# Five transposes of each group leave TensorE: 32x32 blocks turned on VectorE and put in place by DMA through memory, with a new order on every engine

## The reference, cut to what matters

```python
x = layernorm(x + L0(x, adj))   # attention, 8 heads of 16: softmax(q k / 4 + w_e[h] * adj, where adj != 0) v, then W_o
x = layernorm(x + L1(x))        # conv1 -> relu -> 17-tap conv2 -> relu; exp(-distance) @ relu(message); a GRU cell of both
x = layernorm(x + L2(x, adj))   # h = W x + b; adj * exp(e_i + f_j), rows divided by their sums, times h
x = layernorm(x + L3(x, adj))   # graph attention, 4 heads of 32: softmax(leaky(e_i + e_j), where adj > 0) h
```

## Time and profile before

| | |
|---|---|
| median of the executions | 1429.45 us (1429.4 to 1431.82) |
| profiled execution | 1432.08 us, span 1430.3 us |
| mean granted TensorE clock | 0.976 of full speed |
| TensorE matmul busy | 1352.1 us, 95% of the span |
| VectorE busy | 1191.3 us, 83% |
| ScalarE busy | 1188.4 us, 83% |
| GpSimd busy | 663.1 us, 46% |
| DMA | 46.86 MB, 33 GB/s over the span |

### The profile page before, as it was taken

One profiled execution on the slowest core, in us unless ns is written; L12 is line 12 of the kernel. 1 busy time (PEld: TensorE's weight loads), 2 busy tenths in 40 slices (PEclk: granted clock), 3 DMA queues, 4 the chain that ended last, 5 costly groups with the idle time before them and its releaser, 6 DMA issues.

```text
span 1430.3 us, 40514 instructions
## 1 busy us (share of the span) xinstructions
PE 1352.1 (95%) x13178; PEld 1075.1 (75%) x13267; DVE 1191.3 (83%) x3407; ACT 1188.4 (83%) x4353; POOL 663.1 (46%) x1014
## 2 busy tenths in 40 slices
PE   4799999999999999999999999999999999999964
PEld 3577788877778887777888777788877778887642
DVE  6568888888888888888888888888888888886763
ACT  3867888889888888998888899888889988887654
POOL 1133445554444555444455544445554444555532
PEclk7899999999999999999999999999999999999986
DMA  3100110011111001111100111111011111100000
GB/s 117 38 31 31 31 31 17 16 39 38 39 38 39 25 16 39 38 38 39 39 29 12 39 39 38 38 39 34 6 39 39 38 39 38 33 8 16 9 15 23
DMA packets 23825, 46.86 MB, mean 33 GB/s; under 512 B 2753, under 2 KB 2754, under 8 KB 23490
## 3 DMA queue, kind: packets, MB, share of 16 engines
q1 hardware_dynamic: 23618, 44.27, 9.8%
HBM read 35.88 MB, written 8.39 MB: 31 GB/s over the span
## 4 chain that ended last, share of the span: by engine, by line
PE 78%; DVE 10%; POOL 5%; issue 4%; ACT 3%; DVEq 0%; POOLq 0%; ACTq 0%
PE B L591 18%; PE B L689 14%; PE B L499 12%; PE B L537 5%; PE B L558 4%; DVE B L1353 4%; DVE x L1326 3%; POOL rstd L376 3%; PE B L808 2%; PE B L523 2%; PE B L788 2%; PE B L754 2%; PE B L581 2%; PE B L665 2%; PE B L683 2%
## 5 line engine op out<-in xcount | busy, mean ns | idle before, releaser
L995 ACT ACTIVATE e<-B,nm 128x128 f32<-128x128 f32 x1024 | 363.9, 385 | 12.5 <-DVE nm L1361 12.0
L499 PEld LDWEIGHTS B<-ident,e 128*128 128x128 f32 x1536 | 187.0, 144 | 104.3 <-issue 75.7
L499 PE MATMUL B<-ident,e 128*128 128x128 f32 x1536 | 230.0, 281 | 9.2 <-ACT e L1151 3.9
L995 ACT ACTIVATION_READ_ACCUMULATOR e<-B,nm 128x1 f32 x1024 | 231.9, 226 | 0.0
L1353 DVE SCALAR_TENSOR_TENSOR B<-an,rowb,mask 128x512 f32<-128x512 f32 x256 | 194.2, 794 | 19.0 <-ACT pT L1004 9.5
L1151 ACT ACTIVATE e<-l,nm 128x128 f32<-128x128 f32 x512 | 198.9, 400 | 10.0 <-DVE nm L1582 9.9
L1361 DVE TENSOR_REDUCE nm<-B 128x4 f32<-128x512 f32 x256 | 166.5, 683 | 35.0 <-PE B L537 34.8
L1004 ACT ACTIVATE pT<-B 128x512 f32<-128x512 f32 x256 | 157.9, 617 | 44.5 <-PE B L499 41.3
L373 POOL TENSOR_TENSOR veps<-meanv,eps 128x4 f32<-128x4 f32 x128 | 41.8, 326 | 328.9 <-DVE meanv L1320 328.8
L376 POOL TENSOR_TENSOR rstd<-veps,neghalf 128x4 f32<-128x4 f32 x128 | 139.7, 1092 | 10.0
L1582 DVE TENSOR_REDUCE nm<-l 128x4 f32<-128x512 f32 x128 | 87.0, 679 | 41.9 <-ACT l L1141 41.9
(11 more groups left out here) (201 smaller groups left out, 3471.1 us busy)
## 6 DMA issues: line engine op xcount, KB each, us to landing
xt<-in_x_t SPq DMA_DIRECT2D x32, 256.0 KB, 3.1
an<-in_adj_n SPq DMA_DIRECT2D x32, 256.0 KB, 2.7
xn<-in_x_n SPq DMA_DIRECT2D x32, 256.0 KB, 3.3
at<-in_adj_t SPq DMA_DIRECT2D x32, 256.0 KB, 3.2
out_x<-xo SPq DMA_DIRECT2D x32, 256.0 KB, 3.5
wm<-in_mats SPq DMA_DIRECT2D x1, 1088.0 KB, 9.4
wm<-in_mats SPq DMA_DIRECT2D x1, 832.0 KB, 7.1
wm<-in_mats SPq DMA_DIRECT2D x1, 320.0 KB, 3.0
```

What stands on the lines that cost most here:

```text
L499: last = mm(g(dst, b), g(src, b), ident[:, :], is_transpose=True, start=(b == 0), stop=True, skip_group_check=True)
L995: last = fn(g(e0[:, h % 2, :], b), g(bank, b), ACT.Exp, bias=nm0[:, h % 4, b:b + 1], accum_out=sum0[s % 2][:, b, head(h):head(h) + 1])
```

## The change

The five transposes are taken off TensorE and the four copies off ScalarE. A tile that is to be changed over is written by one VectorE `transpose` into a second tile (`x1b`, `x3b`, `yb`, `o3b`; for the output of layer 3 straight from PSUM): each block of 32x32 elements is turned, and the blocks stay where they are. SP then stores that tile to a scratch tensor in memory with one DMA, waits until it has landed, and loads it back with four DMAs, one for each 32 partitions, whose access patterns put each block in its place. They move runs of 32 elements, 128 bytes: 512 of them a DMA, 2048 a tile. For the softmax sums only the 128x32 reciprocals are turned; four DMAs of 32 runs of 128 bytes store them, and one DMA loads them with each row repeated for 16 partitions. `spread_sums` goes from GpSimd. `x1T_ready`, `x3T_ready`, `y_got` and `o3_got` now count 64 a group (`MOVED`).

All orders are new. The lags are different: a group now enters TensorE at t - 5 and leaves VectorE at t - 13, in 45 steps. SP issues 30 DMAs a step in place of 5. The lists of bank users, which follow from the order, are left out below.

```diff
-STEPS = GROUPS + 16
+MOVED = 4 * DMA
+STEPS = GROUPS + 13
...
+            def write_blocks(s, done, sent, got, here, there):
+                if not live(s):
+                    return
+                wait(sp, q[got], MOVED * s)
+                sp.wait_ge(q[done], s + 1)
+                sp.dma_start(there[:, :], here[:, :]).then_inc(q[sent], DMA)
+
+            def read_blocks(s, sent, got, there, here):
+                sp.wait_ge(q[sent], DMA * (s + 1))
+                for c in range(4):
+                    sp.dma_start(here[32 * c:32 * c + 32, :].rearrange("r (b i j) -> r b i j", b=GB, i=4),
+                                 there.rearrange("(i r) (b c j) -> c r b i j", i=4, b=GB, c=4)[c]).then_inc(q[got], DMA)
+
+            def write_sums(s):
...
+                sp.wait_ge(q["rbt_done"], s + 1)
+                for i in range(4):
+                    sp.dma_start(inv_mem.rearrange("h (b i j) -> i (h b) j", b=GB, i=4)[i],
+                                 recb[32 * i:32 * i + 32, :]).then_inc(q["rb_sent"], DMA)
+
+            def read_sums(s):
...
+                sp.wait_ge(q["rb_sent"], MOVED * (s + 1))
+                sp.dma_start(recT[:, :], inv_mem.unsqueeze(1).broadcast_to([H0, D0, GB * N])).then_inc(q["recT_got"], DMA)
...
             def step(t):
+                read_x1(t - 3)
+                write_sums(t - 2)
+                read_sums(t - 2)
+                write_x3(t - 5)
+                write_y(t - 4)
+                read_x3(t - 5)
+                store(t - 9)
                 load_xt(t)
+                load_xn(t - 1)
+                read_y(t - 4)
+                write_out3(t - 6)
+                load_at(t - 2)
+                read_out3(t - 6)
+                write_x1(t - 2)
                 load_an(t)
-                load_xn(t)
-                store(t - 8)
-                load_at(t - 1)
...
+            def turn_x1(s):
+                if not live(s):
+                    return
+                wait(dve, q["x1_sent"], DMA * s)
+                dve.wait_ge(ln_out[0], s + 1)
+                v.transpose(x1b[:, :], x1[:, :]).then_inc(q["x1b_done"], 1)
...
+            def turn_out3(s, bank):
...
+                v.transpose(o3b[:, :], bank[:, :]).then_inc(q["o3b_done"], 1)
```

More of the change, by code:

```diff
@@ L131, in build @@
         x1 = sb("x1", [128, W])
+        x1b = sb("x1b", [128, W])
         x1T = sb("x1T", [128, W])
@@ new lines, in write_x3, with read_x3, write_y, read_y @@
+            def write_x3(s):
+                write_blocks(s, "x3b_done", "x3_sent", "x3T_ready", x3b, x3_mem)
+            def read_x3(s):
+                if not live(s):
+                    return
+                wait(sp, q["h3_ps"], s)
+                wait(sp, q["ej_ps"], s)
+                read_blocks(s, "x3_sent", "x3T_ready", x3_mem, x3T)
+            def write_y(s):
+                write_blocks(s, "yb_done", "y_sent", "y_got", yb, y_mem)
+            def read_y(s):
+                if not live(s):
+                    return
+                wait(sp, ln_out[1], s)
+                read_blocks(s, "y_sent", "y_got", y_mem, yn)
@@ L639, in x1_T @@
                     pe.wait_ge(q["prep"], 1)
[L640 to L647, removed]
+                pe.wait_ge(q["x1T_ready"], MOVED * (s + 1))
                 mm(bank[:, :], wm[:, W1:W1 + N], x1T[:, :], start=True, stop=True).then_inc(q["c1_ps"], 1)
@@ L1488, in gru_out, with turn_y, stats1 @@
                 v.tensor_tensor(yT[:, :], zn[:, :], zx[:, :], ALU.add).then_inc(q["y_done"], 1)
-            def stats1(s, bank):
+            def turn_y(s):
+                if not live(s):
+                    return
+                wait(dve, q["y_sent"], DMA * s)
+                dve.wait_ge(q["y_done"], s + 1)
+                v.transpose(yb[:, :], yT[:, :]).then_inc(q["yb_done"], 1)
+            def stats1(s):
                 if not live(s):
@@ L1572, in norm2, with turn_x3 @@
                     return
-                wait(dve, q["x3t_ps"], s - 1)
+                wait(dve, q["x3b_done"], s - 1)
                 wait(dve, q["r3_done"], s - 1)
                 ln_apply(2, s, r2, x3[s % 2])
+            def turn_x3(s):
+                if not live(s):
+                    return
+                wait(dve, q["x3_sent"], DMA * s)
+                dve.wait_ge(ln_out[2], s + 1)
+                v.transpose(x3b[:, :], x3[s % 2][:, :]).then_inc(q["x3b_done"], 1)
             def row_max3(s, b):
@@ new lines, in step @@
+                norm3(t - 13)
+                hidden_bias(t - 10, (B[1], B[7]))
+                row_max3(t - 11, 0)
+                hidden_times_e(t - 10)
+                row_max3(t - 11, 1)
+                norm1(t - 10)
+                turn_x1(t - 8)
+                edge_mask3(t - 8)
+                row_scales(t - 10, (B[2], B[1]))
+                residual2(t - 10, (B[2], B[1]))
+                half_tanh(t - 9)
+                divide3(t - 12)
+                stats2(t - 10)
+                aggr2(t - 10)
@@ new lines, in step @@
+                edge_mask(t - 6)
+                row_max3(t - 11, 2)
+                reset_hn(t - 9, B[1], B[6], (("pT_ready", 2, 8, 7), ("tr_ready", 0, 1, 1),
+                    ("pT_ready", 2, 8, 5), ("pT_ready", 2, 8, 4), ("v2_done", 0, 1, 1), ("m1_done", 0, 1, 1),
+                    ("n_ready", -1, 1, 1)))
+                invert_sums(t - 7)
+                residual3(t - 12)
+                turn_sums(t - 7)
+                row_max3(t - 11, 3)
+                seed_edges(t - 6, 0, B[0], (("pT_ready", -1, 8, 6), ("l3_done", -5, 4, 1),
+                    ("o3b_done", -6, 1, 1), ("pT_ready", -1, 8, 2), ("exp_done", -1, 8, 1)))
@@ new lines, in step @@
+                norm2(t - 10)
+                turn_x3(t - 10)
+                z_times_n(t - 9)
+                row_max(t - 6, 0, B[0])
+                gru_out(t - 9)
+                row_max(t - 6, 1, B[7])
+                row_max(t - 6, 2, B[4])
+                turn_y(t - 9)
+                divide(t - 7, B[5])
+                message_bias(t - 8, B[6])
+                row_max(t - 6, 3, B[1])
+                shared_to_all(t - 8, B[3])
+                sides(t - 8)
+                residual0(t - 7, B[5])
```

636 lines of the change are left out of this document (281 added, 355 removed).

## The result

The changed kernel takes 1436.9 us in the median of 16 runs (1433.11 to 1444.4), the kernel before 1430.53 us in 16 runs beside them: ratio 1.0047, 95% interval 1.0036 to 1.0058. It is slower by 0.5%, where 1403 us and faster were forecast. The profiled execution has a span of 1434.8 us.

The account below looks back on a forecast made before the run. TensorE's back-to-back work was taken as the bound, 41.6 us a group. 32 periods of 39.7 us (1270.4), plus 99.1 for start, filling and draining and 34 added at the ends, gave about 1403 us; range 1374 to 1458.

Parts of the forecast that it names:

- the list of slacks: Spare time between turn and reader at five places; waits taken as 0.3 us a group (0 to 1.6).
- SP's queue late at x3: Rival: small runs or slow issues on SP hold up targets, 2.2 us a group, 1473 us; chance 0.20.
- The term taken away, 2.2 us a group: TensorE loses five tile turns of 0.44 us each, from 41.6 to 39.4 us a group, 70.4 us in all.
- Nothing else in its work changes; only the order does: Apart from the removed turns, TensorE's work was to stay as it was, 39.4 us a group.
- VectorE's work: Turns add 2.55 us a group, relief from GpSimd takes 1.2 back: 38.1 us of work in 39.4.
- The rival that VectorE becomes the bound: No relief from GpSimd and turns at 0.79 us: period 41.0, 1444 us; chance 0.13.
- x1, y and o3 "hold": Moved tiles reach their readers in time: x1 has 6.2 us for 4.8 of transfer, y and o3 13 us or more.
- Sums "hold by 1.4": From turn_sums to divide, 8.6 us of VectorE's work against 7.2 us of transfer.
- x3 "holds by 0 to 1.1", because of y's store: Tightest place: reads of x3 behind y's store end 7.7 to 8.8 us after the turn, targets needs them at 8.8.
- Adj "holds by 0.7": The load of adj takes 3.1 us, and edge_mask follows 3.8 us after its buffer is free.
- An issue of 0.42 us: Each of 25 more DMA issues a group on SP was taken at 0.42 us, 10.5 us of the 39.4.
- The ends, +34: Filling and draining: 21 us for three change-overs, 8 for filling, 5 for one more step; together 34 (10 to 48).

Follow-up runs that it names:

- e3: The changed kernel with all 25 DMAs a group that move turned tiles and sums left out, readers taking constant tiles: 1379.28 us, ratio 0.9644.
- e4: The changed kernel with the four reads of a tile in 2 KB runs, blocks left unplaced: 1395.94 us, ratio 0.9761.
- e8: The kernel of e6 with the load of adj issued ahead of x1's four stores: 1396.79 us, ratio 0.9765 to the kernel before.
- e7: The kernel before with each of its five tiles turned twice on TensorE: 1486.53 us, ratio 1.0396.
- e9: The kernel of e5 with conv1 ahead of the first scores on TensorE: 1438.96 us, ratio 1.0056 to the kernel before.
- e11: The kernel of e8 with conv1 ahead of the first scores on TensorE: 1418.95 us, ratio 0.9923 to the kernel before.
- e1: The changed kernel with x3's store ahead of recT's load on SP: 1415.02 us, ratio 0.9894 to the kernel before.
- e2: The changed kernel with y's store behind the reads of x3 on SP: 1434.97 us, ratio 1.0033 to the kernel before.
- e10: The kernel of e9 with y's store behind the four reads of x3: 1415.67 us, ratio 0.9904 to the kernel before.
- e6: The changed kernel with blocks placed by four stores, one load reading rows, and y's store behind x3's load: 1436.69 us, ratio 1.0044.
- e5: The kernel of e1 with x1T in two buffers: 1399.33 us, ratio 0.9785 to the kernel before.

## Why the prediction was wrong

The step that failed is the list of slacks: I counted each from its producer and took SP's queue as free, so that the sum had 0.3 us of waits a period. Against the same work without moves (e3) the kernel after has 1.2, because what stands ahead in SP's queue holds the transfers up. The place was in the prediction, as the first rival, "SP's queue late at x3", with a chance of 0.20, but only in part its reasons. It priced small runs as dear for DMA and issues at 1.13 us; measured are 0.65 us an issue, no lack of DMA's capacity (e4, e8), and an order of the queue that the rival doesn't name. In the sum, periods of 41.01 in place of 39.7 cost 32 x 1.31 = 42 us, and the ends gave back 11 of them: 31 us more of span. Point by point:

- **The term taken away, 2.2 us a group: right.** e7 shows 2.2 us of TensorE's work; of a second helping, 1.84 us showed in the period.
- **"Nothing else in its work changes; only the order does": wrong by some 0.6 us.** The period before had 41.65 - 0.23 = 41.4 us without its waits, which less 2.2 is 39.2, and the new order has 39.79 (e3). So TensorE's busy time is 1317.8 us and in e8, without waits, 1310.2, where 1282 was my sign of being right. The timelines show where it lies. A piece of full-size products takes longer next to products on 32 rows or columns (`32*128`, `128*32`). `embed` and the piece behind it, before and in e3:
```profile
732.50 1.06 PE L665 MATMUL B<-wm,x1T 128*128 128x128 f32 x8
733.39 1.02 PE L674 MATMUL B<-lr,ll 128*128 128x512 f32 x2
```
```profile
738.50 1.16 PE L738 MATMUL B<-wm,x1T 128*128 128x128 f32 x8
739.50 0.60 PE L585 MATMUL B<-ident,e 128*128 128x128 f32 x4
```
  From start to start that is 0.89 us before, and 1.00 in e3, where it follows `values`. In the same way `conv1`, between two such pieces, takes 1.06 in place of 0.86, distances and the first piece of `conv_shared` 1 take 0.10 more each, each of three transposes ahead of such products 0.09 more, and `targets`, alone between full ones, 0.36 in place of 0.22. Together 0.9 us a period; the order before had two such stretches in place of four, and about 0.3. e9 and e11 were to take one neighbour away from `conv1`; it kept its 1.05 us (e11), where it stands behind a wait and straight ahead of `scores`. What in the engine makes the difference stays open.
- **VectorE's work: nearly right.** Taken 38.1 us, measured 37.64 (e3). The turn costs 0.63 of the engine, 0.60 was taken. VectorE's busy time rose by 26.5 us, though the turns add 96.5 (22.8 + 22.5 + 22.4 + 22.4 + 6.4): other passes gave back 70 us, about 2 a group, more than the 1.2 taken and the bound of 1.4. The largest parts are the normalisations (25 us), the seeds (18), the edge mask (15) and the sides (10); `residual3` took 6 back. That their distance from GpSimd is the reason was not tested by a run of its own. The rival that VectorE becomes the bound falls. Of the port rule cited from the Trainium skill, "SBUF — State Buffer", section "SBUF: two separate sides": the relief, and `residual3` beside `z_times_x`, agree with it in direction, and the turns, in 700 to 711 ns each, show no stretching in this order.
- **x1, y and o3 "hold": right.** `conv1` waited for x1T in 5 groups, 6.4 us in all, and VectorE for o3n once, 3.6 us.
- **Sums "hold by 1.4": failed.** In the period shown, the way from `turn_sums` to `divide` took VectorE 8.65 us, as counted (8.6), but the transfer took 11.0 and not 7.2. Of the 3.7 us more, 1.8 are SP's: x1's reads, which wait for `z_times_x`, stand ahead. The four stores and their landing take 4.9 and not 3.7, and recT's load 4.2 and not 3.5. `divide` waits for the other 2.3, 51.1 us in all.
- **x3 "holds by 0 to 1.1", because of y's store: place right, reason wrong.** The wait came in 26 groups. What makes it is the store of x3 behind recT's load: issued 2.4 us after its turn and landed in 4.1 us, up to 5.8, where 2.0 to 3.5 were taken. e1 brings it down to 6 groups, and so do the shorter issues of e4 (5 groups); e2 shows that y's store was not it. That y's store matters once the row maxima are late shows only in e9 and e10.
- **Adj "holds by 0.7": right in the kernel after** (one wait, 3.0 us). In e6 2.6 us of issues stand ahead of its load and the mask waits 47.7 / 30 = 1.6, so the slack was about 1.0 us, an estimate.
- **An issue of 0.42 us: wrong, 0.65.** Listed among what would show the forecast wrong, "issues on SP of over 0.6 us". Of the rule cited from the Trainium skill, "DMA: Bandwidth & Descriptors", section "Specifications": by e4, runs of 128 bytes cost 0.5 us more to landing than runs of 2 KB. The dearer part is the issue, 0.2 us each for four.
- **The ends, +34: too much.** +21.1 us measured in the kernel after, of which +8.5 in the filling (8 taken) and 10.7 behind group 31, where 26 were taken. Without moves the draining is 78.3 us (e3), 2.9 less than before, where one step more was to cost 5; the moves then add 13.6, where 21 were taken for three change-overs. Each of them is a little cheaper than I had it: one in the drain, by the chain of waits there, goes 0.72 turn, 2.00 landing, 2.0 for issues, 2.42 landing, 7.4 us from 1389.20 to 1396.58, under my 7.9 to 9.0, because a store that nothing disturbs lands in 2.0. How far y's lies beside other work was not tested.

The forecast of 1403 us is close to what the change gives with its queue in a better order: 1399.3 in e5, 1396.8 in e8. That closeness is partly luck. The work was taken too low (39.4, measured 39.79), and the waits (0.3, none in e8) and the ends too high. The kernel as it was changed gives away 22 us to the place of one store (e1) and 16 more to a single x1T (e5); or 41 to its 128-byte runs (e4), which is the same delay seen from the other side.

## What to carry to other kernels

A slack between a producer and a reader is to be counted along the queue that carries the transfer, with everything ahead of it and what that waits for, and not from the producer alone. Where transfers are many, put a store whose reader is near ahead of a load whose source is still landing, and price an issue by its pattern. If a large change comes out even, run it once with its transfers left out: the difference says at once whether the order of a queue is worth looking at.

## What the runs showed of the hardware

- An issue on SP takes 0.33 us for a store of whole rows, 0.36 to 0.45 for a plain load, and 0.65 us for a quarter tile in 128-byte runs, as a read (after) or as a store (e6). A plain issue right behind four of these is dearer too: 0.62 us for the store of a finished group, 0.42 before and in e4, and 0.55 for the load of adj in e6, 0.33 in e8.
- recT's load, which repeats each row of its source, lands some 4.1 us after its issue (e1), and a store of 256 KB issued right behind it lands after 4.1 us in the median (after), against 2.0 to 2.5 for the other stores of that size. Why this load is slow was not tested.
- 281537 packets under 512 bytes in the kernel after take 34.2% of 16 engines' time; in e8, with 36.5%, TensorE waits for none of them in the period. The small runs cost latency, not throughput.
- A turn of the 32x32 blocks of a 128x512 float32 tile on VectorE takes 700 to 711 ns, from SBUF or PSUM, and 200 ns for 128x32.
- A piece of full-size products on TensorE takes 0.1 to 0.2 us more next to products on 32 rows or columns: `embed` 0.89 us before and 1.00 in e3, `conv1` 0.86 and 1.06. The cause stays open.
- The record of matrix products is not complete: the trace before has 39 of the 128 products of L791, with all 128 of their weight loads. In a TensorE that works back to back this changes the busy time by little, but a group's count and sum can't be compared across traces.
